# Attention on four 32x32 parts of TensorE in whole stages, with ScalarE making three high parts

## The reference, cut to what matters

```python
x = x + xattn(layernorm(x), ctx, Wq, bq, Wk, bk, Wv, bv, Wo, bo)
x = x + ffn(layernorm(x), gate_w, lora_A, lora_B)

# xattn: channels C=128, positions T=1024, heads 8, window 16
q = Wq @ x + bq;  k = Wk @ cond + bk;  v = Wv @ cond + bv
k, v = pad(k), pad(v)                        # 8 left, 7 right
dots = einsum('bhdt,bhdtw->bhtw', qh, k_win) * 16 ** -0.5
attn = softmax(dots, axis=-1)
out  = Wo @ einsum('bhtw,bhdtw->bhdt', attn, v_win) + bo

# ffn: 128 rows per batch, D=1024, rank 64
probs = softmax(x @ gate_w.T); weights, sel = top_k(probs, 2); weights /= sum(weights)
out = sum_e w_full[:, e] * (x @ lora_A[e].T @ lora_B[e].T)
```

## Time and profile before

| | |
|---|---|
| median of 3 runs (lowest to highest) | 1298.94 us (1298.57 to 1300.41) |
| the profiled execution's own time | 1300.73 us |
| its span, first to last instruction | 1298.8 us |
| instructions in the profile | 34642 |
| granted TensorE clock, mean | 0.995 |
| PE, PEld, DVE busy | 1225.5, 1064.8, 891.5 us |
| ACT, POOL busy | 380.5, 416.1 us |

### The profile page before, as it was taken

How to read it: one execution, slowest core, us unless ns; L and a number is a source line. 1 busy time by engine, 2 the same in 40 slices (tenths; PEclk the granted TensorE clock), 3 DMA queues, 4 the chain that set the end, 5 groups by cost and what they waited for, 6 DMA issues and landing times.

```text
span 1298.8 us, 34642 instructions
## 1 busy us (share of the span) xinstructions
PE 1225.5 (94%) x13953; PEld 1064.8 (82%) x14080; DVE 891.5 (69%) x2021; ACT 380.5 (29%) x553; POOL 416.1 (32%) x300
## 2 busy tenths in 40 slices
PE   3889999999999999999999999999999999999986
PEld 2778888888888888888888888888888888888875
DVE  3777667766767766767766767776767766767653
ACT  3332232322232322232322232322232322232211
POOL 3443333323333332332323333322332322333110
PEclk9989999999999999999999999999999999999999
DMA  6443433343443343443343443243443343443210
GB/s 214 79 88 67 99 91 75 83 90 62 97 91 81 77 97 64 88 93 75 81 95 60 95 92 88 70 99 67 83 93 87 70 99 64 85 93 76 58 40 33
DMA packets 427427, 108.44 MB, mean 83 GB/s; under 512 B 410001, under 2 KB 410129, under 8 KB 427153
## 3 DMA queue, kind: packets, MB, share of 16 engines
q1 hardware_dynamic: 427280, 106.13, 37.6%
HBM read 55.22 MB, written 16.78 MB: 55 GB/s over the span
## 4 chain that ended last, share of the span: by engine, by line
PE 91%; issue 3%; DVE 1%; DMA 1%; POOL 1%; SPq 1%; ACT 0%; POOLq 0%; DVEq 0%
PE bank_a L318 30%; PE bank_b L350 22%; PE bank_b L363 19%; PE bank_c L318 16%; PE bank_a L373 4%; DMA v_diag<-v_t 1%; POOL src_split L873 0%; SPq L237 0%; SPq L246 0%; POOL v_diag L878 0%; DMA ident<-ident_in 0%; DMA raw<-ctx 0%; DVE mid_split L767 0%; DMA q_diag<-q_xn 0%; POOL src_split L883 0%
## 5 line engine op out<-in xcount | busy, mean ns | idle before, releaser
L350 PE MATMUL bank_b<-k_sb,q_diag 64*64 64x32 f32 x8192 | 312.5, 222 | 31.2 <-issue 30.9
L350 PEld LDWEIGHTS bank_b<-k_sb,q_diag 64*64 64x64 f32 x8192 | 271.0, 136 | 83.9 <-issue 71.7
L363 PEld LDWEIGHTS bank_b<-prob_t,v_diag 128*128 128x128 f32 x2304 | 315.7, 192 | 23.8 <-DMA v_diag<-v_t 4.9
L363 PE MATMUL bank_b<-prob_t,v_diag 128*128 128x96 f32 (+2 forms) x2304 | 326.9, 270 | 4.6 <-DMA v_diag<-v_t 4.6
L318 PE MATMUL bank_a<-down_split,mid_split 128*128 128x264 f32 (+1 forms) x1536 | 267.5, 298 | 2.7 <-DVE mid_split L767 2.7
L867 POOL TENSOR_TENSOR prob<-prob,row_inv 128x512 f32<-128x512 f32 x128 | 146.4, 1144 | 323.4 <-DVE row_inv L726 323.4
L318 PE MATMUL bank_c<-src_split,w_split 128*128 128x512 f32 x576 | 221.1, 459 | 18.0 <-POOL src_split L873 14.2
L318 PEld LDWEIGHTS bank_a<-down_split,mid_split 128*128 128x128 f32 x1536 | 214.9, 189 | 15.9 <-ACT mid_split L548 3.0
L318 PE MATMUL bank_a<-up_split,ht_split 128*128 128x512 f32 x768 | 216.3, 405 | 4.0 <-DVE ht_split L808 3.6
L318 PEld LDWEIGHTS bank_a<-up_split,ht_split 128*128 128x128 f32 x768 | 138.2, 189 | 33.8 <-ACT ht_split L585 4.2
L733 DVE STREAM_TRANSPOSE prob_t<-prob 128x768 f32<-128x768 f32 x128 | 124.6, 973 | 30.4 <-POOL prob L867 30.4
(11 more groups left out here) (68 smaller groups left out, 1087.1 us busy)
## 6 DMA issues: line engine op xcount, KB each, us to landing
v_diag<-v_t SPq DMA_DIRECT2D x128, 132.0 KB, 3.8
raw<-x SPq DMA_DIRECT2D x32, 512.0 KB, 5.9
raw<-ctx SPq DMA_DIRECT2D x32, 512.0 KB, 3.4
q_diag<-q_xn SPq DMA_DIRECT2D x512, 32.0 KB, 2.4
resid_pair<-x SPq DMA_DIRECT2D x32, 512.0 KB, 3.4
out<-resid_pair SPq DMA_DIRECT2D x32, 512.0 KB, 2.6
v_diag<-up_w SPq DMA_DIRECT2D x1, 2048.0 KB, 9.3
prob_t<-down_w SPq DMA_DIRECT2D x1, 780.0 KB, 4.8
```

The lines of the kernel that those rows point to most:

```text
L350: last = nc.tensor.matmul(bank_b[m % 2][rows, t * KT:(t + 1) * KT], q_diag[rows, m // 2, n, :], k_sb[rows, at:at + KT], start=False, stop= ...
L363: last = nc.tensor.matmul(bank_b[2 + m % 2][:, lo * PW:hi * PW], v_diag[:, n * P:(n + 1) * P], prob_t[:, at:at + (hi - lo) * KT], start=i ...
```

## The change

Scores are computed on four 32x32 parts, one for each pair of heads: 256 products a batch instead of 128, each with 32 columns of weights. The weighted values too: 256 products of 32x32 instead of 36 of 128x128. The block-diagonal `v_diag` goes; in its place the transposed values lie in two buffers, `v_even` as VectorE writes them, and `v_odd`, in which eight DMAs swap the halves of each pair of rows and shift by one block for tiles of odd number. `prob` and `prob_t` lose their gaps (512 columns a chunk instead of 768). `q_diag`, `k_sb`, `v_even`, `v_odd` and `attn` exist once per parity of the batch, `q_sb`, `xn2` and `attn_split` are buffers of their own, and so several waits go.

TensorE's work is no longer interleaved in quarters: a stage is a whole projection, a whole half of `down`, or `attend`, which does a chunk of scores and then a chunk of weighted values. ScalarE instead of VectorE makes the high parts of the normalised x (`xn_hi`), of ctx (`ctx_hi`) and of the attention rows (`attn_hi`). GpSimd's and VectorE's lists are in another order, and in the DMA queue `place_q` now stands ahead of the load of the next x.

```diff
-            def place_v():
-                blocks = v_diag[:].rearrange("p (n c) -> p n c", c=P)
+            def place_v(cur):
+                half = PW // 2
+                source, odd = v_even[cur.parity], v_odd[cur.parity]
                 for g in range(PAIRS):
-                    rows = slice(PW * g, PW * (g + 1))
-                    sp.dma_start(blocks[rows, :, PW * g:PW * (g + 1)],
-                                 v_t[rows, :].rearrange("p (n c) -> p n c", c=PW)).then_inc(v_placed, 16)
+                    low = slice(PW * g, PW * g + half)
+                    high = slice(PW * g + half, PW * (g + 1))
+                    sp.dma_start(odd[low, :], source[high, 0:T]).then_inc(v_placed, 16)
+                    sp.dma_start(odd[high, :], source[low, KT:KT + T]).then_inc(v_placed, 16)
...
+            def scores_chunk(cur, m):
+                keys = k_sb[cur.parity]
+                for t in range(CT):
+                    n = m * CT + t
+                    for g in range(PAIRS):
+                        rows = slice(PW * g, PW * (g + 1))
+                        last = nc.tensor.matmul(bank_b[m % 2][rows, t * KT:(t + 1) * KT],
+                                                q_diag[rows, cur.parity, n, :],
+                                                keys[rows, n * QT:n * QT + KT], start=False,
+                                                stop=t == CT - 1, skip_group_check=True)
+                last.then_inc(scores_done, 1)
...
+            def weighted_chunk(b, m):
+                for t in range(CT):
+                    n = m * CT + t
+                    values = (v_even, v_odd)[n % 2][b.parity][:, n // 2 * PW:(n // 2 + 1) * PW]
+                    at = n * PW
+                    for g in range(PAIRS):
+                        rows = slice(PW * g, PW * (g + 1))
+                        last = nc.tensor.matmul(bank_b[2 + m % 2][rows, t * PW:(t + 1) * PW],
+                                                values[rows], prob_t[rows, at:at + PW],
+                                                start=t == 0, stop=t == CT - 1, skip_group_check=True)
+                last.then_inc(pv_done, 1)
...
+                def attend(m, weighted, k):
+                    if weighted:
+                        open_weighted(weighted, k)
+                    if cur:
+                        if m == 0:
+                            pe.wait_ge(q_placed, cur.count(16 * HEADS, 16 * HEADS))
+                        open_scores(cur, m)
+                        scores_chunk(cur, m)
+                    if weighted:
+                        weighted_chunk(weighted, k)
+
                 if cur:
                     pe.wait_ge(k_out, cur.count(1, 1))
+                    for n in range(6):
+                        last = project_pass(n, bank_c, 2, src_split)
+                    last.then_inc(v_done, 1)
+                attend(0, prev, 2)
...                                          # transposes of xn2
+                attend(1, prev, 3)
...                                          # Q projection, then down(0, all)
+                attend(2, cur, 0)
...                                          # O projection, then down(1, all)
+                attend(3, cur, 1)
...                                          # transposes of h_sb, K projection, up
@@ ScalarE's step
+                if ahead:
+                    act.wait_ge(xn_done, ahead.count(1, 1))
+                    nc.scalar.activation(src_split[:, 0, :], raw[:], ACT.Copy).then_inc(xn_hi, 1)
...
+                if prev:
+                    act.wait_ge(attn_done, prev.count(CHUNKS, CHUNKS))
+                    nc.scalar.activation(attn_split[:, 0, :], attn[prev.parity], ACT.Copy).then_inc(attn_hi, 1)
+                if ahead:
+                    act.wait_ge(raw_in, ahead.count(32, 32))
+                    nc.scalar.activation(src_split[:, 0, :], raw[:], ACT.Copy).then_inc(ctx_hi, 1)
@@ VectorE's step
-                    nc.vector.tensor_copy(src_split[:, 0, :], raw[:]).then_inc(xn_hi, 1)
-                    nc.vector.tensor_copy(src_split[:, 0, :], raw[:]).then_inc(ctx_hi, 1)
-                    nc.vector.tensor_copy(mid_split[:, 0, :], attn[:]).then_inc(attn_hi, 1)
```

More of the change, by code:

```diff
@@ L163, in build @@
         pads_zero = sem("pads_zero")
[L164 removed]
+        q_diag_zero = sem("q_diag_zero")
         raw_in = sem("raw_in")
@@ new lines, in step @@
+                attend(1, prev, 3)
+                if ahead:
+                    pe.wait_ge(xn_hi, ahead.count(1, 1))
+                    pe.wait_ge(xn_lo, ahead.count(1, 1))
+                    if cur:
+                        pe.wait_ge(v_out, cur.count(1, 1))
+                    for n in range(6):
+                        last = project_pass(n, bank_c, 0, src_split)
+                    last.then_inc(q_done, 1)
+                if old:
+                    pe.wait_ge(xt_hi, old.count(2, 2))
+                    pe.wait_ge(xt_lo, old.count(2, 2))
+                    if old.c == 0:
+                        pe.wait_ge(weights_lo, 5)
+                    for f in range(FK):
+                        down(0, f)
@@ new lines, in step @@
+                attend(2, cur, 0)
+                if prev:
+                    pe.wait_ge(attn_hi, prev.count(1, 1))
+                    pe.wait_ge(attn_lo, prev.count(1, 1))
+                    if ahead:
+                        pe.wait_ge(q_out, ahead.count(1, 1))
+                    elif cur:
+                        pe.wait_ge(v_out, cur.count(1, 1))
+                    for n in range(6):
+                        last = project_pass(n, bank_c, 3, attn_split)
+                        if n % 3 == 2:
+                            last.then_inc(o_done, 1)
@@ new lines, in step @@
+                if old:
+                    for f in range(FK):
+                        down(1, f)
+                attend(3, cur, 1)
+                if old:
+                    pe.wait_ge(h_done, old.count(2, 2))
+                    transposes(bank_a, h_sb, range(EK)).then_inc(ht_done, 1)
+                if ahead:
+                    pe.wait_ge(ctx_hi, ahead.count(1, 1))
+                    pe.wait_ge(ctx_lo, ahead.count(1, 1))
+                    if prev:
+                        pe.wait_ge(x1_done, prev.count(2, 2))
+                    else:
+                        pe.wait_ge(q_out, ahead.count(1, 1))
+                    for n in range(6):
+                        last = project_pass(n, bank_c, 1, src_split)
+                    last.then_inc(k_done, 1)
```

357 lines of the change are left out of this document (105 added, 252 removed).

## The result

The changed kernel takes 1604.03 us (median of 4 runs, 1600.24 to 1612.33), the kernel before 1298.83 on the same chip: ratio 1.2355, 95% interval 1.2305 to 1.2406. It is slower by 305 us, where 1174 us was predicted.

The account below looks back on a forecast made before the run. TensorE was taken as the bound at 39.0 us a step, then a chain of engines at 35.1: 3.9 us times 32 is 125, 1300.7 - 125 = 1176, less 1.8 gives 1174 us. Forecast 1125 to 1215, range 1090 to 1270.

Parts of the forecast that it names:

- The price of four parts: Attention's scores and values: four passes on four 32x32 parts load side by side in 0.032 us, a chunk takes 1.02.
- (a): TensorE stays the bound, the four parts take turns in twos, 0.058 us for four: 1264 us; chance 0.14.
- (b): No overlap of passes beyond today's mean, 0.029 us each: step 52.7 us, 1737 in all; chance 0.11, skill's floor included.
- its 1610: Time if matmul starts never come closer than about 25 ns: chunk 3.2 us, step 48.7; chance counted within (b).
- Dense work: Projections, `down`, `up` and transposes on TensorE: 20.7 us a step, left as it is by the change.
- Copies: VectorE loses three copies, 2.1 us, and falls to 24.5 us a step; ScalarE gains three, reaching 14.8; POOL unchanged.
- The chain at 34.7 us: A step's chain through VectorE, ScalarE and POOL to the end of `up`, with the loop's jump: 34.7 us.
- the 31.2 us step: TensorE's own work in a step after the change: 20.7 + 8.2 + 1.3 + 0.5 + 0.5 us.
- Rival (c): Instructions arrive late for attention's chunks: 9.0 us more a step, 1337 us, or 1193 if half are early; chance 0.12.
- the 35.1 us step: The step forecast: the chain's 34.7 us plus about ten handovers between engines at some 0.04 each.
- The clock: Sign that the forecast is wrong: a clock below full because PE now pauses; no size given.
- 0.5 + 0.5 as predicted: TensorE per step: leaving the small parts 4 times instead of 12, 0.5 us, and the loop's jump, 0.5.

Follow-up runs that it names:

- whole4_unroll: Kernel before with scores on four 32x32 parts and whole chunks instead of quarters, every step of the loop written out: 1202.78 us, ratio 0.925.
- whole64_unroll: Kernel before with its 64x64 parts kept but whole chunks instead of quarters, every step of the loop written out: 1248.41 us, ratio 0.963.
- pause experiment: Kernel before, with TensorE waiting once a step for a small DMA that ScalarE starts after `down`: 1537.97 us, ratio 1.183.

## Why the prediction was wrong, step by step

*The price of four parts: right.* 0.032 us was predicted for four passes, 0.035 measured (1.11 / 32, were read rightly). Rivals (a), turns in twos, and (b), no overlap, fell: a chunk of 1.11 us leaves no room for either. The floor of about 25 ns from start to start that the Trainium skill gives ("TensorE: Matmul & The Clock Gate", section "Wait — 56ns, not 53.3ns?") does not hold between parts: here a pass starts every 8.7 ns. That its 1610 lies beside the measured 1604 is chance: its chunk would last 3.2 us, and the trace's lasts 1.11 where nothing pauses. The Trainium skill's rule that tiles "can execute LdWeights and Matmul in parallel" ("TensorEngine Tiling (Array Packing)", section "Key Properties") is the one that the trace bears out.

*Dense work: mis-sized to the other side.* 20.7 us was carried over from interleaved stages. At full clock `down` costs 0.123 a pass ((717.63 - 714.67) / 24 in `whole4_unroll`), `up` 0.230 ((733.31 - 729.86) / 15), a projection 0.228: 5.9 + 5.5 + 5.5 + 1.3 = 18.2.

*Copies: right for ScalarE, and without weight.* ACT 28.8 / 2 = 14.4 us a step (14.8 predicted), POOL 12.3. VectorE has 26.2 (24.5 predicted), so it lost 1.4 us and not 3.0: two small operations, the cast at L620 and the shift at L597, last 0.95 and 0.37 us where they took 0.18 and 0.16, 1.2 us a step; why is open.

*The chain at 34.7 us: never reached.* TensorE had not the 31.2 us step that would have exposed it. VectorE does wait for POOL before the transposes, but in a step that TensorE sets; whether 34.7 would have bound was not tested.

*Rival (c), instructions don't arrive: the step that failed.* The mechanism stood in the text, with 9.0 us a step, and got 0.12. The argument against it, "no stall of that kind is seen", was read from a trace that never asked: before, a step of 39 us used 136 / 32 = 4.3 packets, one per 9 us. Two sizes were wrong. A packet was priced at twice its transfer, 2.14 us, from the earlier trace rows; a PE that waits gets one per 3.5 to 4.1. Some of them are in store when a burst begins (bursts of 256 mostly run through), and the measured pauses are 11.0 us a step, not 9.0. And the mean need, 311 / 32 = 9.7 packets a step, is 34 to 40 us at that pace: by itself about the 35.1 us step that I predicted. The bursts come on top. That I had 256 instructions to a packet was luck: 34642 / 136 divides the instructions of all engines. PE's 28160 matmuls and loads are 110 packets, and the other 26 go with the loop (`whole64_unroll`, with the same products, fetches 111).

*The clock: not priced at all.* It was named among the signs and had no term. The ledger of a step: 18.2 dense + 8 x 1.11 = 8.9 chunks + 1.3 masks + 0.5 + 0.5 as predicted = 29.4; pauses 11.0: 40.4. The step takes 48.7, and 8.3 are left, for a clock of 0.77 over the step and small gaps; a projection alone pays 2.72 - 1.37 = 1.35. Rival (c) with its size mended would have said 31.2 + 11.0 = 42.2, or 1401 us; the 6.5 us a step that it still lacks are these 8.3, less the cheaper dense work (2.5) and with the dearer chunks (0.7). The pause experiment shows that a clock cost of this order follows pauses; how much of the 8.3 is something else stays open.

## What to carry to other kernels

Before work is cut into smaller instructions, count instructions per us in the densest microseconds, not their mean: here a waiting PE was fed 256 instructions per 3.5 to 4.1 us, and bursts of 256 mostly ran through where bursts of 512 stopped. A resource that has never been asked for is not shown to be plentiful; price it with the clock that a waiting TensorE loses, which here added 3.4 us to a pause of 4.5. And where a kernel is dense in instructions, try the same steps written out: that gained 88 and 50 us here, and nothing where it was not dense.

## What the runs showed of the hardware that I had not expected

- Four 32x32 parts take a pass each 8.7 ns (1.11 us for 128), loads included.
- A TensorE that waits for instructions gets 256 per 3.5 to 4.1 us, in a loop (median 4.02) and in straight code (4.12) alike, though the transfer of a packet takes 1.0 to 1.1 and the DMA engines may be idle otherwise.
- A loop's jump back costs about two instruction packets (25 or 26 for 13 turns). Written out, the same steps took 88, 50, 10 and 0 us less.
- 64x64 parts with 96 moving columns gain nothing here over 128x128 products: 0.40 to 0.48 us instead of 0.36 for a group, +3.5% and +8.0% for the kernels.
- Whole stages of one kind are cheaper than interleaved ones: a pass of `down` 0.123 instead of 0.152 us; whole chunks alone gave 4%.
